# Cross-attention in row bands, its clamp on GpSimd, and segment attention in half-array tiles

## The reference

```
x = L0_xattn(x, ctx, mask)           # 16 heads of 8 dims, 128 queries x 77 keys
    scores = q k^T / sqrt(8);  scores = 0.5*(scores*mask) + 0.5*scores
    scores = clip(scores, -50, 50);  attn = softmax(scores);  context = attn v
    x = layernorm(x + context Wo + bo) * gamma + beta
x = L1_xattn(x, ctx, ...)            # 16 heads of 64 dims, segments of 64 tokens
    xn = rms_norm(x);  q, k, v = split(xn @ to_qkv_w);  q, k = rope(q), rope(k)
    keys = 16 equal memory tokens + 16 persistent tokens + the causal part of the own segment
    x = x + softmax(q k^T / 8) v @ to_out_w
    x = x + (silu(g) * a) @ ff_w2 + ff_b2,  a, g = split(rms_norm(x) @ ff_w1 + ff_b1)
```

## Time and profile before

| | |
|---|---|
| median of 3 runs | 1803.2 us (1799.8 to 1804.67) |
| profiled execution: span from its first to its last instruction | 1801.7 us |
| one pass of the loop (start of L905 to the next one) | 27.25 us |
| PE busy, PEld busy | 1666.4 us (92%), 1434.9 us (80%) |
| DVE busy | 1543.8 us (86%) |
| ACT busy | 1073.9 us (60%) |
| POOL busy | 856.9 us (48%) |
| mean granted TensorE clock | 0.997 |

### The profile page before, as it was taken

The page is one execution under the profiler, slowest core; times in us unless marked ns, Lnnn a source line. Parts: engine busy times, 40 slices in busy tenths (PEclk is TensorE's granted clock), DMA queues, the critical chain, the costliest instruction groups (busy, mean ns, idle before and its releaser), DMA issues.

```text
span 1801.7 us, 52360 instructions
## 1 busy us (share of the span) xinstructions
PE 1666.4 (92%) x17891; PEld 1434.9 (80%) x17891; DVE 1543.8 (86%) x3730; ACT 1073.9 (60%) x2637; POOL 856.9 (48%) x1107
## 2 busy tenths in 40 slices
PE   4899999999999999999999999999999999999997
PEld 3788788788888887888888888887888888878876
DVE  5788888889889889888888888888888898898894
ACT  3555656655656656656556556566566556566563
POOL 4344534535535535445445445445355355355352
PEclk9999999999999999999999999999999999999999
DMA  6000000000000000000000000000000000000000
GB/s 176 17 9 11 10 10 11 8 13 11 8 13 11 8 13 11 8 11 12 8 11 13 8 11 13 8 11 8 12 11 8 13 11 8 13 11 8 13 6 6
DMA packets 32411, 26.14 MB, mean 15 GB/s; under 512 B 8118, under 2 KB 31179, under 8 KB 32139
## 3 DMA queue, kind: packets, MB, share of 16 engines
q1 hardware_dynamic: 32394, 25.93, 5.4%
HBM read 21.46 MB, written 4.46 MB: 14 GB/s over the span
## 4 chain that ended last, share of the span: by engine, by line
DVE 49%; PE 22%; issue 21%; ACT 3%; POOL 3%; DVEq 1%; DMA 1%; SPq 0%; ACTq 0%; POOLq 0%
DVE z L658 9%; PE psum L927 6%; DVE ra L641 5%; DVE z L650 5%; DVE rb L644 5%; DVE mx L730 4%; PE psum L854 4%; DVE rden L662 3%; PE psum L898 3%; DVE sT L752 3%; DVE o L676 3%; DVE c0T L668 2%; ACT z L523 2%; POOL st L464 2%; DVE y L770 1%
## 5 line engine op out<-in xcount | busy, mean ns | idle before, releaser
L409 POOL TENSOR_TENSOR ra<-ra,rb 128x512 f32<-128x512 f32 x256 | 332.2, 1324 | 0.2
L464 POOL TENSOR_TENSOR st<-st,nhalf 128x1 f32<-128x1 f32 x64 | 38.3, 598 | 535.4 <-DVE st L763 535.4
L872 PE MATMUL psum<-qpad,kall 128*81 128x128 f32 x2048 | 251.6, 276 | 0.0
L641 DVE TENSOR_TENSOR ra<-psum,rope 128x512 f32<-128x512 f32 x256 | 174.3, 681 | 77.9 <-PE psum L838 77.8
L872 PEld LDWEIGHTS psum<-qpad,kall 128*81 128x81 f32 x2048 | 224.9, 151 | 2.6
L658 DVE TENSOR_SCALAR z<-z 77x512 f32<-77x512 f32 x256 | 216.8, 885 | 0.0
L581 ACT ACTIVATE probs<-psum 81x512 f32<-81x512 f32 x256 | 131.3, 593 | 142.3 <-PE psum L880 142.3
L523 ACT ACTIVATE z<-z 77x512 f32<-77x512 f32 x256 | 154.1, 627 | 67.1 <-DVE z L658 65.5
L854 PE MATMUL psum<-z,v 77*64 77x128 f32 x2048 | 141.6, 280 | 44.9 <-ACT z L523 44.9
L644 DVE TENSOR_TENSOR rb<-psum,rope 128x512 f32<-128x512 f32 x256 | 173.0, 676 | 0.0
L836 PE MATMUL psum<-wqkv_hi,xnT_hi 128*128 128x512 f32 x384 | 168.6, 439 | 2.7 <-DVE xnT_lo L681 1.8
(11 more groups left out here) (141 smaller groups left out, 4028.3 us busy)
## 6 DMA issues: line engine op xcount, KB each, us to landing
seq_in<-in SPq DMA_DIRECT2D x64, 166.5 KB
out<-out_sb SPq DMA_DIRECT2D x64, 64.0 KB, 1.6
maskT<-in SPq DMA_DIRECT2D x64, 38.5 KB
vall<-memv_dram SPq DMA_DIRECT2D x128, 4.0 KB, 1.9
ctx_all<-in SPq DMA_DIRECT2D x5, 320.0 KB, 12.3
wqkv<-in SPq DMA_DIRECT2D x1, 1536.0 KB, 10.1
stage<-in SPq DMA_DIRECT2D x1, 1296.0 KB
ctx_all<-in SPq DMA_DIRECT2D x3, 288.0 KB, 11.3
```

The lines of the kernel that those rows point to most:

```text
L409: nc.gpsimd.tensor_tensor(ra[:, sl], ra[:, sl], rb[:, sl], ALU.add).then_inc(rot_ready, 1)
L641: V.tensor_tensor(ra[:, sl].rearrange("n (h d) -> n h d", h=8), p, rope[:, 0, :].unsqueeze(1).broadcast_to([S, 8, DH]), ALU.mult)
L872: mm(self_at(f"score{t}")[0:KEYS, 128 * n:128 * (n + 1)], kall[:, pair, s, :], qpad[:, pair, s, :, :].rearrange("p h i -> p (h i)"), start ...
```

## The change

Cross scores. Keys alone are masked, once by `head % 4` (`kmask`, POOL), in float32. Group g's heads lie in rows 32g to 32g+31, so a head's scores are a product over one band of 32 rows; groups 0 and 1 alternate, then 2 and 3, each group in a bank of its own. The hi and lo parts are gone, with ACT's and POOL's work for them. The clamp moves from DVE to POOL, two clamps before the sums for q1 and k1 and two behind them.

Cross context. Products write bands of 32 columns: one product with `v0` (32 columns, zeros but for the head's 8) gives the context, one with `ones0` the sums at the same partitions, 32 products instead of 16, all into one task pv. DVE takes one reciprocal and makes one multiplication.

Segment attention. `qT` holds the turned queries without padding, one ACT copy per half instead of two. The estimate of the maxima is 32 products of 64 rows x 64 columns, `scores` 32 products over 64 rows (81 columns, 64 queries), two heads of a pair in turn and in different banks. `less_maxima` is 16 products of 128 columns. The maxima's two parts take one DVE instruction each. The shift lies in a spare part of the bank of `gate`, and waits for its reader.

```diff
@@ POOL
-            pool.wait_ge(qk0_ready, c + 1)
-            nc.gpsimd.tensor_tensor(q0T_rest[:], q0T[:], q0T_hi[:].bitcast(F32), ALU.subtract)
-            nc.gpsimd.tensor_tensor(k0T_rest[:], k0T[:], k0T_hi[:].bitcast(F32), ALU.subtract).then_inc(rest0_step, 1)
-            pool.wait_ge(rest0_step, c + 1)
-            lower(1)
...
-            lower(0).then_inc(lo0_ready, 1)
...
-            for name in QK:
-                rotated(name)
+        def clamped(t):
+            lim = CLAMP * float(HD0) ** 0.5
+            zt = z0[:, 4 * t:4 * t + 4, :]
+            pool.wait_ge(z_ready, c * 4 + (t + 1))
+            passed(pool, pool_passed)
+            nc.gpsimd.tensor_scalar(zt, zt, lim, -lim, ALU.min, ALU.max).then_inc(clip_ready, 1)
...
+            pool.wait_ge(k0_ready, c + 1)
+            nc.gpsimd.tensor_tensor(kmask[:], headmask.unsqueeze(2).broadcast_to([D, GROUP, S2]),
+                                    k0T[:].unsqueeze(1).broadcast_to([D, GROUP, S2]), ALU.mult).then_inc(kmask_ready, 1)
@@ ACT
-            copy(qpad[rows, 4 * t:4 * t + 4, :, h, :],
+            copy(qT[:, 4 * t:4 * t + 4, :].rearrange("p c i -> p (c i)"), self_at(f"q{t}T")).then_inc(q_ready, 1)
@@ DVE
-                masked(0)
-                masked(1)
-                clamped(0)
-                clamped(1)
-                masked(2)
-                masked(3)
-                clamped(2)
-                clamped(3)
+                for t in range(4):
+                    masked(t)
...
+            def context_sums():
+                wait(dve, cross_filled("pv", c))
+                V.reciprocal(rden0[:], cross_at("pv")[:, S:2 * S]).then_inc(cross_step, 1)
+            def context():
+                wait(dve, (cross_step, cross_steps[1]("rden0", c)))
+                V.tensor_tensor(c0T[:], cross_at("pv")[:, 0:S], rden0[:], ALU.mult).then_inc(c0T_ready, 1)
@@ PE
+                def cross_scores(*groups):
+                    for g in groups:
+                        wait(pe, cross_free(f"score{g}", c))
+                    for r in range(GROUP):
+                        for g in groups:
+                            rows = slice(32 * g, 32 * (g + 1))
+                            last = mm(cross_at(f"score{g}")[0:S2, S * r:S * (r + 1)], kmask[rows, r, :], q0T[rows, :], start=r == 0)
+                            if r == GROUP - 1:
+                                last.then_inc(cross_fill(f"score{g}"), 1)
+                def weigh_cross(*groups):
+                    for r in range(GROUP):
+                        window = slice(32 * r, 32 * (r + 1))
+                        for g in groups:
+                            mm(cross_at("pv")[32 * g:32 * (g + 1), 0:S], v0[:, g, window], z0[:, 4 * g + r, :], start=r == 0)
+                        for g in groups:
+                            last = mm(cross_at("pv")[32 * g:32 * (g + 1), S:2 * S], ones0[:, window], z0[:, 4 * g + r, :], start=False)
+                    return last
...
+                def scores(half):
+                    wait(pe, self_free(f"score{2 * half + 1}", a))
+                    for n in range(4):
+                        for s in range(NSEG):
+                            for h in range(2):
+                                t, dims = 2 * half + h, slice(DH * h, DH * (h + 1))
+                                mm(self_at(f"score{t}")[0:KEYS, S * n + SEG * s:S * n + SEG * (s + 1)], kall[dims, 4 * half + n, s, :],
+                                   qT[dims, 4 * half + n, SEG * s:SEG * (s + 1)], start=n == 0 and s == 0, stop=False)
```

More of the change, by code:

```diff
@@ L158, in build @@
         k0T = sb("k0T", [D, S2])
[L160 to L165 removed]
+        kmask = sb("kmask", [D, GROUP, S2])
+        v0 = sb("v0", [S2, GROUP, GROUP * VROW])
+        ones0 = sb("ones0", [S2, GROUP * VROW])
         z0 = sb("z0", [S2, H, S])
[L167 removed]
+        rden0 = sb("rden0", [128, S])
         c0T = sb("c0T", [D, S])
@@ L596, in _ @@
             dve.wait_ge(cross_w_in, CROSS_WEIGHTS_IN)
-            for which, bias in ((0, BQ), (1, BK)):
-                V.tensor_scalar(head_bias[:, which, :], headmask[:, which, :], cols[:, bias:bias + 1], None, ALU.mult)
             dve.wait_ge(setup_pe, 1)
@@ L865, in turn, with maxima @@
                     last.then_inc(self_fill(f"{name}T"), 1)
-                def scores(t):
-                    wait(pe, self_free(f"score{t}", a))
-                    for n in range(4):
-                        pair, s = 2 * t + n // 2, n % 2
-                        mm(self_at(f"score{t}")[0:KEYS, 128 * n:128 * (n + 1)], kall[:, pair, s, :],
-                           qpad[:, pair, s, :, :].rearrange("p h i -> p (h i)"), start=n == 0, stop=False)
+                def maxima(half):
+                    if half == 1:
+                        wait(pe, self_free("max3", a))
+                    for t in (2 * half, 2 * half + 1):
+                        p = self_at(f"max{t}")[:, 0:4 * KEYS].rearrange("i (n k) -> i n k", n=4)
+                        mm(p[:, :, 0:SEG], ident_b[:], causal_b[:].unsqueeze(1).broadcast_to([128, 4, SEG]), stop=False)
+                    for n in range(4):
+                        for h in range(2):
+                            t, dims = 2 * half + h, slice(DH * h, DH * (h + 1))
+                            for s in range(NSEG):
+                                queries = slice(SEG * s, SEG * (s + 1))
+                                last = mm(self_at(f"max{t}")[queries, KEYS * n:KEYS * (n + 1)], q_upper[dims, 4 * half + n, queries],
+                                          k_upper[dims, 4 * half + n, s, :], start=False)
+                            if n == 3:
+                                last.then_inc(self_fill(f"max{t}"), 1)
@@ L875, in less_maxima @@
                 def less_maxima(t):
                     for n in range(4):
-                        pair, s = 2 * t + n // 2, n % 2
-                        p = self_at(f"score{t}")[0:KEYS, 128 * n:128 * (n + 1)]
-                        for h in range(2):
-                            last = mm(p[:, SEG * h:SEG * (h + 1)], select_b[:, (2 * pair + h) * NSEG + s, :], shift_b[:], start=False)
+                        last = mm(self_at(f"score{t}")[0:KEYS, S * n:S * (n + 1)], select_b[:, 4 * t + n, :], shift_b[:], start=False)
@@ L963, in body @@
                 if c is not None:
-                    weigh_cross(0)
-                    weigh_cross(1)
+                    wait(pe, cross_free("pv", c))
+                    pe.wait_ge(exp0_ready, c * 4 + 2)
+                    weigh_cross(0, 1)
+                    pe.wait_ge(exp0_ready, c * 4 + 4)
+                    weigh_cross(2, 3).then_inc(cross_fill("pv"), 1)
                 if a is not None:
```

219 lines of the change are left out of this document (75 added, 144 removed).

## The result

| | before | changed |
|---|---|---|
| median of the runs | 1801.85 us (4 runs, 1799.80 to 1804.67) | 1788.69 us (4 runs, 1787.39 to 1791.21) |
| ratio, 95% interval | 1 | 0.9924 [0.9908, 0.9940] |
| span of the profiled execution | 1801.7 us | 1787.0 us |
| usual pass (distance between the starts of the first transposes) | 27.24 us | 27.03 us |

The account below looks back on a forecast made before the run. It took one chain from engine to engine, no engine alone, as the bound. Its terms, 9.15 + 8.83 + 9.60 = 27.58 us a pass against 27.25, add 20.8 us over 63 passes: 1824 us, 1.2% slower, range 1768 to 1900.

Parts of the forecast that it names:

- r: VectorE operation before the second `normalised`, forecast to start 5.27 us after the maxima start, 6.01 in the kernel before.
- row bands: Segment `scores` on TensorE: two row bands run side by side, so a pass costs 0.036 us.
- the change of shape: TensorE switching tile shape: 0.09 us more each, seven changes on the chain, two there before.
- T to M: From VectorE ending `rotary` and beginning `masked` (T) to the start of the maxima (M): 8.83 us against 7.66.
- M to X: From the start of the maxima (M) to the next pass's first transpose (X): 9.60 us, 0.75 less.
- A pass under 27.2: Listed sign that the forecast of a slightly longer pass, 27.58 us against 27.25, is wrong.
- The term of the maxima: After M: per half two causal products, a shape change and 16 passes at 0.030, together 0.78 us.
- `weigh_cross` with the step to M: End of T to M: 64 passes at 0.0545 us, 3.49, plus 0.11 to the maxima.
- X to T: From a pass's first transpose (X) to VectorE beginning `masked` (T): 9.15 us, 0.09 off for a shorter square sum.
- the rival built on it: A change of shape empties the array: 0.07 us more for seven changes, pass 28.07, 1855 us; chance 0.08.
- GpSimd clamps as fast as VectorE: Clamp of 0.41 us on GpSimd: T to M 8.35, pass 27.10, 1794 us, faster; chance 0.25.
- Its second half: Same rival, if shape changes also cost nothing and four small tiles overlap: pass 26.67, 1766 us; within the 0.25.

Follow-up runs that it names:

- experiments 1: The changed kernel with GpSimd's four sums (q0, k0, q1, k1) ahead of all four clamps: 1731.33 us, ratio 0.9618.
- experiment 2: The changed kernel with its clamps back on VectorE in their old places, the rest kept: 1730.69 us, ratio 0.9606.
- experiment 3: The changed kernel with segment scores ordered so that neighbours in the queue share a row band: 1941.92 us in one run.
- experiment 8: The changed kernel with each half of the maxima run with the row band outermost, so neighbours share one: 1789.89 us, ratio 0.9933.
- experiment 4: The changed kernel with all four groups of `weigh_cross` at once, behind the fourth exponential: 1790.38 us in one run.
- experiment 7: The changed kernel with sums before clamps, maxima and first scores before four-group `weigh_cross`, q1 and v1 copies before exponentials 2 and 3: 1753.65 us, ratio 0.9646.
- (9): The kernel of experiment 7 with its TensorE stall filled by eight products of the identity with itself that compute nothing: 1762.72 us, ratio 0.9774.
- (10): The kernel of experiment 7 with key copies moved earlier and the first maxima waiting for the first keys alone: 1650.88 us, ratio 0.9172.

## Why the prediction was wrong

**The mechanism was right in the main.** GpSimd's queue, TensorE's stall before the third `turn` (0.76 us, forecast 0.9), VectorE's share (67%, forecast 65), its idle time of over 2 us before the maxima (3.14), the pass that still waits for `normalised`, and an r that comes a good 0.7 us earlier (it was 1.05) are in the trace, and experiments 1 and 2 move the time exactly there. Prices that held, forecast first: row bands 0.036 us (0.036), one row band by itself 0.072 (0.072 in experiment 3), the change of shape 0.09 (0.10: from the last row of L826, at 952.72 + 0.63 - 0.28 = 953.07, to 953.28 it is 0.21, over the spacing of 0.11), the clamp 0.65 (0.60). The working given for 0.072 does not lead to it, since 0.060 x 81/64 is 0.076; that it held is luck.

**The sum was 0.55 us a pass too high**, 27.58 against 27.03, and the gain or loss to be told was only 0.2 to 0.3. The forecast had T to M lose 1.17 us and M to X gain 0.75; measured, T to M lost 0.82 and M to X gained 1.05, and the sign turned over. A pass under 27.2 was the prediction's own first sign of being wrong. The steps that failed are terms of the sum that were mis-sized:

- *M to X, 9.60, measured 9.30.* The term of the maxima, 0.78 us per half, was mis-sized. Half 0 starts at 929.46 and half 1 at 930.08: 0.62 each. The passes inside cost 0.010 us, where I took 0.030 from an fp32 row and the kernel before had a bf16 one (experiment 8). TensorE no longer holds up the last two reduces, and VectorE makes all four without a gap, from M + 0.72 to M + 2.42, where I had 2.72. So the shift starts 2.98 us after M and not 3.27, and r 4.96 and not 5.27. From r to X it is 4.34 us, as forecast (4.33). The wait of 0.37 us for the bank of the first scores was not in my list; it fell in time that the shift would have waited for VectorE in any case.
- *T to M, 8.83, measured 8.48.* Up to the start of `weigh_cross` the sum held, 5.23 against 953.28 - 948.02 = 5.26: the two clamps were 0.13 shorter (1.17), and the step from the first mask to the first clamp, 0.88 for 0.74, gave it back. The term that failed is `weigh_cross` with the step to M, 64 x 0.0545 + 0.11 = 3.60, measured 956.50 - 953.28 = 3.22. The sum took two bands throughout, but at the seam of the halves four run together, which saves 0.39 (experiment 4, which shows the same at full length). That covers the whole of the 0.35.
- *X to T, 9.15, measured 9.26.* The square sum of x1 did get short, as guessed (0.29 us for 0.51), but the normalisation after it (`hn`) takes 0.70 us, with GpSimd's sums beside all of it, and had taken 0.60. The 0.09 us that I took off went back, and this error hid a sixth of the others.

By the Trainium skill, "TensorEngine Tiling (Array Packing)", Key Properties, a change of tiling mode drains the array; the rival built on it forecast 1855 us. The spacing at the first row of `weigh_cross` shows 0.10 us over the usual one, not the 0.164 of a full emptying, and the kernel was faster: here the measurement stands against that price, which was the prediction's, not against a cost as such. The estimate from the Trainium skill, "GPSIMD Engine Reference", section 3.1, 769 ns for 512 elements, was 1839 us; the clamp measured 0.61 us, its fixed part included.

**The rival that came nearest** is "GpSimd clamps as fast as VectorE", with 1794 us, but its condition (a clamp of 0.41 us) is not what happened. Its second half asked for two things: shape changes were not free (0.10), but four small tiles did overlap, at the seam of `weigh_cross`. I gave both halves together 0.25. That the time fell inside the range is no merit of the sum: the range was wide enough for most rivals (its lower end, 1768, leaves out the 1766 that it claims to take in). The bounds of the terms allowed the outcome: two column bands or four, 0.0545 or half of it, was never bounded, and the maxima were taken at one value without ends.

## What to carry to other kernels

Moving work to an idle engine moves it into a queue: ask what stands behind it there, and put first what the bottleneck waits for. When a change removes a fifth of an engine's work and the time hardly falls, look for the gain as idle time in front of that engine's next operation, and reorder the producers in front of that wait (here 27.03 to 24.87 us) before removing more. And when the gain to be told is 1% of a pass, each term must be right to a tenth of that, so the sign deserves less confidence than its mechanism.

## What the runs showed of the hardware

- Four column bands of fp32 products with 128 columns cost 0.027 us each, two 0.0545: the bands scale to four. Where one group of products in two bands ends and the next, in the two others, begins, both run together, 16 passes in 0.48 us, though the code issues the second group behind the first. Products of 64 rows of bf16 with 81 columns cost 0.010 to 0.012 us each, whether two bands or four tiles are neighbours.
- The granted clock can fall to about 1.2 GHz for some 10 us in a loop in which TensorE is never idle for more than 1.1 us at a time (experiments 4 and 7). Filling the stall of experiment 7 (9) or removing it (10) ended this. That speaks for the idle time as what lets the clock fall, but does not show it alone: the stall stands in every pass of experiment 7 and only 9 of 62 are long, mostly five passes apart, and experiments 9 and 10 also changed the length of the pass and ran on another chip. Padding a pass without filling its stall was not tried. The Trainium skill, "TensorE: Matmul & The Clock Gate", section "A second HAM failure mode: psum-queue depth-cycling", tells of a kernel in which short idle times of TensorE between groups of products let its clock go to and fro; experiments 4, 7, 9 and 10 agree with it as far as they go. Experiment 3 does not fit as plainly: its longest wait is no longer than that of the changed kernel, TensorE is busier in it, and the clock still fell in every sixth pass,

```profile
341.79:373.25 31.46, 30.12 (x363) 26.58 (x364) 18.75 (x49) 12.06 (x29) 12.90 (x18) 0.89 0.03 9
...
312.93:341.79 28.86, 26.94 (x364) 23.48 (x364) 18.64 (x49) 12.06 (x29) 12.91 (x18) 1.00 0.04 10
```

and why stays open. It was one run.
- One clamp of 77 x 512 takes 0.60 us on GpSimd. On VectorE it took 0.92 beside GpSimd's sums, and takes 0.46 and 0.51 in experiment 2, where the sums have ended or nearly so. For this operation with one input the two engines are closer than the 1.30 us of GpSimd's two-input sum suggests, and VectorE's price depends on what GpSimd does meanwhile.
